# Cross-attention and feed-forward in fp32 on one core: row maxima taken in pairs on half-height matmuls, and the last feed-forward chunk in two halves

## The chip, the cores and the metric

The kernel runs on one NeuronCore of one Trainium2 chip. The metric is the device time of one execution in microseconds (us), lower is better. The median of three runs of the kernel before is 789.1 us (788.37 to 789.65).

## The reference, cut to what matters

Four residual layers are applied one after the other to x (4 x 1024 rows of 256 features), each to a layer-normed input:

```
x = x + attention0(layernorm(x), ctx, mask)   # 16 heads of 16, 77 keys a batch, biases, a mask
x = x + experts(layernorm(x))                 # 6 experts of 128, top 2, tanh gelu
x = x + attention1(layernorm(x), ctx, ctx)    # 16 heads share one key and one value head; q @ k.T / 4
x = x + ffn(layernorm(x))                     # 256 -> 1024 -> 256, piecewise-linear gelu on 33 points,
                                              # values rounded to multiples of 1/256
```

Both attentions use a softmax, so each query row needs its maximum over 77 keys for each head before the exponential.

## The kernel before, in words

The 4096 rows are 8 blocks of 512. A stage runs over all blocks before the next begins: attention 0 (blocks G = 0 to 7), the experts, attention 1 (G = 8 to 15), the feed-forward. Each engine has its own instruction list, written out by hand; semaphores order the engines, and within an engine the order is the program's. All matmuls on the main path split their operands into a leading and a rest part (fp32r) and use three products for one.

A block of attention works like this, with the work for the next block n = G + 1 woven in.

- TensorE makes 16 score tiles (`score`, L400, one for each head, 77 keys x 512 queries). In attention 0 a second matmul (L416) adds the mask. The stationary operand is a stacked key, the moving one a stack of the query's leading part twice, its rest, and minus the row maximum. The maximum is a row of that stack, so no score of block n can start before the row maxima of block n have come in by a DMA (`stack_maxima`, L260, on SyncE's queue).
- ScalarE takes the exponential of each score tile (`exp`, L312).
- TensorE weighs the values (`weigh`, L419): four heads go to four 32-column strips of the array, as 8 matmuls with a 128x32 stationary operand. VectorE turns the result (`unfold`), divides (`divide`) and turns it back (`fold`). TensorE applies the output weights (`output`, L429, 12 matmuls for each half), and VectorE adds to x (`add`).
- For block n, TensorE makes the queries (`queries`, L374, six matmuls for each of two feature halves c), ScalarE and VectorE split them (`leading`, `rest`), and then come 16 units of row maxima (`max_unit`, L378). A unit is one tile of 128 queries against four heads: one matmul of 128x128 against 308 columns (4 heads x 77 keys, from `kblk`, where each head's key stands in its own rows and all other rows are zero), and in attention 0 a second one (L391) that adds the mask. It fills one PSUM bank. VectorE then reduces 308 columns to 4 maxima (`take_maxima`, L335). Units take turns on two banks, `att.X`, so unit u waits until VectorE has taken unit u - 2.
- After the 16 units TensorE turns the maxima (`turn_maxima`, L394, four matmuls), ScalarE copies them (`maxima`, L307) and the DMA puts them into the stack: the next block's first score waits for that.
- The first block of each attention takes its maxima before the loop, over four banks (`FIRST_MAX`, `FIRST_MAX1`).

Within a partition the features are laid out so that rows 0 to 63 hold the even heads of a feature half and rows 64 to 127 the odd ones.

In the feed-forward a block has 8 chunks of 128 hidden features, 64 chunks in all. A chunk k passes: TensorE `hidden`; VectorE `early` (fixed point); ScalarE `gelus` (two activations); GpSimd `climb` (the difference, L721); VectorE `interpolate` (L768); GpSimd `grow` (L728) or VectorE `finish` (the sum); ScalarE `leading` (two activations, L745 and L748); VectorE `rest` (L780); TensorE `output` (12 matmuls, L812). After a block's eight chunks ScalarE rounds (`round_output`), VectorE adds to x (`add`, L789) and SyncE stores the block (L978). The end of the program is this chain for chunk 63 and the store of block 7.

Of the kernel before, what the change touches and what calls it, by code (L numbers as in the profile page):

```python
# [166 lines left out]
class Attention:  # L167


    def __init__(self, nc, sem, place, norm, ps, m):  # L170
        self.nc, self.norm = nc, norm
        self.W, self.X, self.SC, self.U = ps[0:2], ps[2:4], (ps[4], ps[5], ps[7]), ps[6]
# [162 lines left out]
    def take_maxima(self, dve, G, units, banks):  # L335
        for u in units:
            t, c, half = u // 4, u % 4 // 2, u % 2
            dve.wait_ge(self.max_scores, 16 * G + u + 1)
            if u == 0:
                need(dve, self.mt_done, G)  # L340
            out = self.mx[:, t, :].rearrange("q (par c p) -> q c p par", par=2, c=C)[:, c, 2 * half:2 * half + 2, :]
            self.nc.vector.reduce_max(out, banks[u % len(banks)][:, 0:4 * T].rearrange("q (p par t) -> q p par t", p=2, par=2),  # L342
                                      AX.X).then_inc(self.max_taken, 1)
# [34 lines left out]
    def max_unit(self, pe, layer, G, u, banks):  # L378
        t, c, half = u // 4, u % 4 // 2, u % 2
        pe.wait_ge(self.qh_ready, C * G + c + 1)  # L380
        if u == 0:
            need(pe, self.mt_ready, G)
        if u >= len(banks):
            pe.wait_ge(self.max_taken, 16 * G + u - len(banks) + 1)
        bank = banks[u % len(banks)][:, 0:4 * T]
        tile = slice(t * P, (t + 1) * P)
        keys = layer.kblk[:, c % layer.kc, self.batch(G), 4 * half:4 * half + 4, :]
        last = self.nc.tensor.matmul(bank, self.qh[:, c, tile], keys, start=True, stop=not layer.masked)  # L388
        if layer.masked:
            pe.wait_ge(self.mask_ready, 3 * G + 1)  # L390
            last = self.nc.tensor.matmul(bank, self.mh[:, tile], self.id5[:, 0:4 * T], start=False, stop=True)  # L391
        last.then_inc(self.max_scores, 1)

    def turn_maxima(self, pe, G, bank):  # L394
        pe.wait_ge(self.max_taken, 16 * (G + 1))
# [258 lines left out]
class FeedForward:  # L654
# [5 lines left out]
    def __init__(self, nc, sem, place, norm, ps, m):  # L660
# [46 lines left out]
        self.stored = sem("fstored")  # L707

    def wait_y(self, eng, k):

        if k >= 0:
            g, c = divmod(k, FC)
            mine = [j for j in range(FC) if (j in self.ON_DVE) == (c in self.ON_DVE)]
            eng.wait_ge(self.y_ready[c in self.ON_DVE], len(mine) * g + mine.index(c) + 1)

# [34 lines left out]
    def round_output(self, act, g):  # L750
        act.wait_ge(self.used, FC * (g + 1))
        for k in range(2):
            bank = self.OUT[2 * (g % 2) + k]
# [87 lines left out]
def build(nc, d, out):  # L841
    m, at0, at1 = memory_map()
    place = Places(nc)
    with ExitStack() as stack:
# [3 lines left out]
        ps = [stack.enter_context(nc.psum_tensor(f"bank{i}", [P, N], F32)) for i in range(8)]  # L848
# [6 lines left out]
        att = Attention(nc, sem, place, norm, ps, m)  # L855
# [34 lines left out]
        UNITS1 = {1: (0,), 2: (1,), 3: (2,), 4: (3,), 5: (4, 5), 6: (6, 7), 7: (8, 9), 9: (10,), 10: (11,), 11: (14, 15)}  # L890
        FIRST_MAX = (ps[2], ps[3], ps[6], ps[7])
        FIRST_MAX1 = (ps[6], ps[7], ps[2], ps[3])

        with nc.Block() as block:
            @block.sync
            def _(sp):
# [79 lines left out]
                for g in range(BLOCKS):  # L976
                    sp.wait_ge(ff.added, 2 * (g + 1))
                    sp.dma_start(out[:, g * NT:(g + 1) * NT, :], x[:, g * NT:(g + 1) * NT, :]).then_inc(ff.stored, 16)  # L978
                sp.wait_ge(ff.stored, 16 * BLOCKS)

            @block.gpsimd
            def _(pool):
# [120 lines left out]
                for k in range(BLOCKS * FC):  # L1103
                    g, c = divmod(k, FC)
                    ff.climb(pool, k)
# [4 lines left out]
                if FC - 1 not in ff.ON_DVE:  # L1110
                    ff.grow(pool, BLOCKS * FC - 1)

            @block.scalar
            def _(act):
# [22 lines left out]
                att.maxima(act, 0, FIRST_MAX[0])  # L1137
# [12 lines left out]
                for G in range(BLOCKS):  # L1150
                    p, n, nm = G - 1, G + 1, G + 2
                    for h in range(H):
# [3 lines left out]
                        if h == 2 and p >= 0:  # L1156
# [5 lines left out]
                        if h == 5 and p >= 0:  # L1162
                            att.lead_quotient(act, p, 1)
                        if h == 9 and nm <= BLOCKS:
                            norm.norm(act, nm)
                        if h == 12 and n < BLOCKS:
                            att.maxima(act, n, att.X[0])
# [45 lines left out]
                att.maxima(act, BLOCKS, FIRST_MAX1[0])  # L1213
# [3 lines left out]
                for G in range(BLOCKS, 2 * BLOCKS):  # L1217
                    p, n, nm = G - 1, G + 1, LN_ATT1 + G - BLOCKS + 2
                    for h in range(H):
                        att.exp(act, G, h)  # L1220
                        if h < C and n < 2 * BLOCKS:
                            att.leading(act, n, h)
                        if h == 2 and p >= BLOCKS:
# [7 lines left out]
                        if h == 12 and n < 2 * BLOCKS:  # L1231
                            att.maxima(act, n, att.X[0])
# [22 lines left out]
                for k in range(BLOCKS * FC):  # L1255
# [5 lines left out]
                    if k > 0:  # L1261
# [15 lines left out]
                for k in range(BLOCKS * FC - 3, BLOCKS * FC):  # L1277
                    ff.leading(act, k)
                ff.round_output(act, BLOCKS - 1)

            @block.vector
            def _(dve):
# [6 lines left out]
                for c in range(C):  # L1289
                    dve.wait_ge(k_done, c + 1)  # L1290
                    nc.vector.tensor_scalar(l0.kt[:, c, :], FIRST_MAX[2 + c][:, 0:BT], att.cols[:, 1, c:c + 1], DH ** -0.5,
# [14 lines left out]
                att.take_maxima(dve, 0, range(16), FIRST_MAX)  # L1306
# [4 lines left out]
                for G in range(BLOCKS):  # L1311
# [8 lines left out]
                    if n < BLOCKS:  # L1320
                        for c in range(C):
                            att.rest(dve, n, c)
                        att.take_maxima(dve, n, range(0, 2), att.X)
                    if p >= 0:
                        att.unfold(dve, p, 3)
                    if n < BLOCKS:
                        att.take_maxima(dve, n, range(2, 4), att.X)
                    if p >= 0:
                        att.divide(dve, p, 1)
                    if n < BLOCKS:  # L1330
                        att.take_maxima(dve, n, range(4, 6), att.X)
                    if p >= 0:
                        att.fold(dve, p, 1)
                    if n < BLOCKS:
                        att.take_maxima(dve, n, range(6, 10), att.X)
# [3 lines left out]
                    if n < BLOCKS:  # L1339
                        att.take_maxima(dve, n, range(10, 12), att.X)  # L1340
                    if p >= 0:
                        att.add(dve, p, 0)
                    if n < BLOCKS:
                        att.take_maxima(dve, n, range(12, 16), att.X)
                    if p >= 0:
                        att.add(dve, p, 1)
# [426 lines left out]
```

## Time and profile before

| | |
|---|---|
| median of three runs | 789.1 us |
| profiled execution | 788.65 us |
| its span, first to last instruction | 786.4 us |
| PE busy | 730.7 us (93%) |
| DVE busy | 645.4 us (82%) |
| ACT busy | 513.6 us (65%) |
| POOL busy | 374.3 us (48%) |
| mean granted TensorE clock | 0.99 of 2.4 GHz |

PE is TensorE's matmuls, DVE VectorE, ACT ScalarE, POOL GpSimd, SP SyncE. A matmul's row gives a modelled length that is longer than its place in the stream: the distance from one start to the next is what it costs. Attention 0 runs from about 41 to 210 us, attention 1 from about 415 to 577 us, the feed-forward after that.

### The profile page before, as it was taken

The page shows a single profiled execution, that of the slowest core. Times are in us where ns is not written, and L with a number is a line of the kernel's source. Part 1 is how long each engine was busy: PE and PEld are TensorE (multiplying, and loading weights), DVE is VectorE, ACT ScalarE, POOL GpSimd, SP SyncE. Part 2 cuts the span into 40 slices and gives each one's busy share as a digit, 9 for nine tenths or more (in the row PEclk, how much of TensorE's full clock was granted, in tenths as well). Part 3 has the DMA queues.
Part 4 walks back from the last instruction along what each step waited for, and adds up shares of the span by engine and source line. Part 5 has one row for each costly group of instructions (what it writes and reads, how often), then busy time and mean ns, then how long its engine had stood idle before and what let it go on. Part 6 is the DMA issues. An engine that isn't in the chain of part 4 may idle for free.

```text
span 786.4 us, 13553 instructions
## 1 busy us (share of the span) xinstructions
PE 730.7 (93%) x4372; PEld 548.4 (70%) x4372; DVE 645.4 (82%) x1546; ACT 513.6 (65%) x943; POOL 374.3 (48%) x323
## 2 busy tenths in 40 slices
PE   4799999999999999999998999999989999999995
PEld 3456666766558888888875555555558888888985
DVE  7658778777878878888887888998788999999995
ACT  3546556565654456555436777677778989989885
POOL 6374444334222223232214232222259999999884
PEclk9999999999999999999999999999999999999999
DMA  7975635564210000001047755755200000000001
GB/s 231 135 208 121 143 71 96 119 120 87 69 36 1 1 1 7 1 1 55 1 60 121 92 78 77 131 76 78 32 1 1 2 28 28 28 28 2 28 28 54
DMA packets 25101, 48.64 MB, mean 62 GB/s; under 512 B 3686, under 2 KB 7016, under 8 KB 24520
## 3 DMA queue, kind: packets, MB, share of 16 engines
q1 hardware_dynamic: 23366, 46.54, 30.6%
q10 hardware_dynamic: 1666, 1.24, 0.5%
q8 instruction: 36, 0.59, 0.3%
q14 instruction: 33, 0.27, 0.2%
HBM read 12.12 MB, written 4.19 MB: 21 GB/s over the span
## 4 chain that ended last, share of the span: by engine, by line
PE 53%; DVE 20%; issue 9%; ACT 7%; DMA 6%; POOL 4%; DVEq 0%; ACTq 0%; POOLq 0%
PE bank L141 15%; PE bank L649 7%; PE bank L413 6%; PE bank L436 6%; DMA qst<-mt 5%; PE bank L424 5%; PE bank L388 4%; DVE mx L342 4%; PE bank L416 3%; PE bank L812 3%; DVE fpart L768 3%; DVE x L617 2%; PE bank L391 2%; DVE fyl L780 2%; POOL fy L728 2%
## 5 line engine op out<-in xcount | busy, mean ns | idle before, releaser
L316 ACT ACTIVATE pt<-bank 77x512 f32<-77x512 f32 x256 | 141.0, 589 | 79.1 <-PE bank L416 59.3
L342 DVE TENSOR_REDUCE mx<-bank 128x4 f32<-128x308 f32 x256 | 108.6, 470 | 22.9 <-PE bank L391 12.3
L413 PE MATMUL bank<-qst,l_kst 128*77 128x512 f32 (+1 forms) x256 | 102.6, 416 | 16.8 <-DMA qst<-mt 10.5
L721 POOL TENSOR_TENSOR frise<-fg,fg 128x512 f32<-128x512 f32 x64 | 101.8, 1591 | 6.0 <-DVE fpart L768 0.8
L388 PE MATMUL bank<-l_kblk,qh 128*128 128x308 f32 x256 | 81.2, 339 | 7.6 <-DVE mx L342 6.4
L284 POOL TENSOR_TENSOR ol<-ot,oh 128x512 fp32r<-128x512 f32 x32 | 41.4, 1293 | 94.5 <-ACT oh L321 50.4
L103 POOL TENSOR_TENSOR rstd<-var,minus_half 128x4 f32<-128x4 f32 x32 | 34.8, 1088 | 102.5 <-DVE var L98 54.4
L617 DVE SCALAR_TENSOR_TENSOR x<-bank,eweight,x 128x256 f32<-128x256 f32 x192 | 79.5, 475 | 4.5 <-PE bank L649 4.2
L413 PEld LDWEIGHTS bank<-qst,l_kst 128*77 128x77 f32 (+1 forms) x256 | 36.5, 146 | 66.0 <-ACT pt L316 24.1
L114 ACT ACTIVATE xn<-x,shift,rstd 128x256 f32<-128x256 f32 (+1 forms) x128 | 67.0, 592 | 17.9 <-POOL shift L105 17.9
L812 PE MATMUL bank<-fw2h,fyh 128*128 128x256 f32 x256 | 73.3, 286 | 5.0 <-DVE fyl L780 4.7
L388 PEld LDWEIGHTS bank<-l_kblk,qh 128*128 128x128 f32 x256 | 47.6, 190 | 41.3 <-issue 33.6
L728 POOL TENSOR_TENSOR fy<-fpart,fg 128x512 f32<-128x512 f32 x48 | 68.5, 1428 | 9.8 <-DVE fpart L768 6.8
L812 PE MATMUL bank<-fw2l,fyh 128*128 128x256 f32 x256 | 72.0, 281 | 0.0
L812 PE MATMUL bank<-fw2h,fyl 128*128 128x256 f32 x256 | 71.9, 281 | 0.0
L424 PE MATMUL bank<-pt,l_vall 128*32 128x512 f32 x512 | 68.2, 604 | 1.3 <-DVE ut L347 0.9
L768 DVE SCALAR_TENSOR_TENSOR fpart<-ffixed,frise 128x512 f32<-128x512 uint16 x64 | 58.3, 911 | 12.4 <-POOL frise L721 12.4
L649 PE MATMUL bank<-ew2h,ehh 128*128 128x256 f32 x192 | 56.5, 294 | 2.8 <-DVE x L617 2.8
L518 POOL TENSOR_TENSOR ehl<-eh,ehh 128x512 fp32r<-128x512 f32 x16 | 20.7, 1293 | 80.7 <-ACT ehh L534 80.7
L812 PEld LDWEIGHTS bank<-fw2h,fyh 128*128 128x128 f32 x256 | 48.2, 188 | 11.0 <-DVE fyl L780 9.0
L649 PE MATMUL bank<-ew2l,ehh 128*128 128x256 f32 x192 | 54.6, 285 | 0.0
L532 ACT ACTIVATE eh<-bank 128x512 f32<-128x512 f32 x48 | 28.7, 597 | 39.6 <-PE bank L141 38.5
(176 smaller groups left out, 2115.6 us busy)
## 6 DMA issues: line engine op xcount, KB each, us to landing
qst<-qh SPq DMA_DIRECT2D x64, 256.0 KB, 6.5
qst<-ql SPq DMA_DIRECT2D x32, 256.0 KB, 8.7
out<-x SPq DMA_DIRECT2D x8, 512.0 KB, 2.6
qst<-ml SPq DMA_DIRECT2D x8, 480.0 KB
x<-in_x SPq DMA_DIRECT2D x3, 1024.0 KB, 12.7
weights<-in_mlp_w SPq DMA_DIRECT2D x2, 1024.0 KB, 5.2
mraw<-in_mask SPq DMA_DIRECT2D x8, 154.0 KB
x<-in_x SPq DMA_DIRECT2D x2, 512.0 KB, 5.4
```

The lines of the kernel that those rows point to most:

```text
L141: last = self.nc.tensor.matmul(out, w, a, start=(first and k == 0), stop=(k == len(ops) - 1))
L316: self.nc.scalar.activation(self.pt[0:T, i // 4 % 2, i % 4, :], self.bank_of(G, i)[0:T, :], ACT.Exp).then_inc(self.probs, 1)
L342: self.nc.vector.reduce_max(out, banks[u % len(banks)][:, 0:4 * T].rearrange("q (p par t) -> q p par t", p=2, par=2), AX.X).then_inc(self. ...
L388: last = self.nc.tensor.matmul(bank, self.qh[:, c, tile], keys, start=True, stop=not layer.masked)
L413: last = self.nc.tensor.matmul(out, layer.kst[rows, layer.stack(c * HC + 2 * k + par), b * T:(b + 1) * T], self.qst[rows, self.slot(G), c ...
L424: last = self.nc.tensor.matmul(self.U[32 * k:32 * k + 32, :], layer.vall[:, self.batch(G), layer.value(c * HC + 2 * k + par), :], self.pt[ ...
L617: last = self.nc.vector.scalar_tensor_tensor(tile, part, self.weight[:, g % 2, 2 * k + t, e:e + 1], tile, ALU.mult, ALU.add)
L649: last = self.nc.tensor.matmul(self.OUT[k][:, t * D:(t + 1) * D], a[:, e % self.R, tile], w[:, e, :], start=(j == 0), stop=(j == 2))
L721: self.nc.gpsimd.tensor_tensor(self.rise[:, k % 2, :], self.g1[:, k % self.R, :], self.g0[:, k % self.R, :], ALU.subtract).then_inc(self.r ...
L728: self.nc.gpsimd.tensor_tensor(self.y[:, k % 2, :], self.part[:, k % 2, :], self.g0[:, k % self.R, :], ALU.add).then_inc(self.y_ready[0], 1)
L768: self.nc.vector.scalar_tensor_tensor(self.part[:, k % 2, :], self.fractions[:, k % self.R, :, 0], 2.0 ** -16, self.rise[:, k % 2, :], ALU ...
L812: last = nc.tensor.matmul(self.OUT[2 * (g % 2) + t // 2][:, t % 2 * D:(t % 2 + 1) * D], a[:, k % self.R, t * P:(t + 1) * P], w[:, c, :], s ...
```

## The change

- The units become pairs. `max_pair` computes one query tile against eight heads: one matmul on rows 0 to 63 with the four even heads into the first bank of a pair of banks, one on rows 64 to 127 with the four odd heads into the second bank; in attention 0 two full-height mask matmuls follow. VectorE reduces both banks, 616 columns, in one instruction. Eight pairs replace 16 units. The loops have one pair of banks (2 and 3), so pair v waits until pair v - 1 has been taken; before the loops there are two pairs of banks.
- The order of work within the blocks is changed: in attention 0 both query halves come after score 1, the last weighing of the block before after score 3, the first output after score 11, and the third weighing after score 14 instead of 15. In attention 1 the first query half comes ahead of score 0 (for blocks 9 to 14), the first weighing after score 6, and on VectorE the layer norm's rest comes before `fold`.
- Chunk 63 goes through all steps in two halves of 256 columns, with its difference and its sum on VectorE instead of GpSimd; the last block is stored in two parts.

```
-    def max_unit(self, pe, layer, G, u, banks):
-        t, c, half = u // 4, u % 4 // 2, u % 2
+    def max_pair(self, pe, layer, G, v, banks):
+        t, c = divmod(v, C)
...
-        bank = banks[u % len(banks)][:, 0:4 * T]
-        tile = slice(t * P, (t + 1) * P)
-        keys = layer.kblk[:, c % layer.kc, self.batch(G), 4 * half:4 * half + 4, :]
-        last = self.nc.tensor.matmul(bank, self.qh[:, c, tile], keys, start=True, stop=not layer.masked)
+        if v >= len(banks):
+            pe.wait_ge(self.max_taken, 8 * G + v - len(banks) + 1)
+        pair = banks[v % len(banks)]
+        tile = slice(t * P, (t + 1) * P)
+        for par in range(2):
+            half = slice(64 * par, 64 * par + 64)
+            last = self.nc.tensor.matmul(pair[:, par, 0:4 * T], self.qh[half, c, tile],
+                                         layer.kblk[half, c % layer.kc, self.batch(G), 4 * par:4 * par + 4, :],
+                                         start=True, stop=not layer.masked)
         if layer.masked:
-            pe.wait_ge(self.mask_ready, 3 * G + 1)
-            last = self.nc.tensor.matmul(bank, self.mh[:, tile], self.id5[:, 0:4 * T], start=False, stop=True)
+            for par in range(2):
+                last = self.nc.tensor.matmul(pair[:, par, 0:4 * T], self.mh[:, tile], self.id5[:, 0:4 * T], start=False, stop=True)
         last.then_inc(self.max_scores, 1)
...
-            self.nc.vector.reduce_max(out, banks[u % len(banks)][:, 0:4 * T].rearrange("q (p par t) -> q p par t", p=2, par=2),
+            self.nc.vector.reduce_max(out, banks[v % len(banks)][:, :, 0:4 * T].rearrange("q par (p t) -> q par p t", t=T),
                                       AX.X).then_inc(self.max_taken, 1)
...
-        UNITS1 = {1: (0,), 2: (1,), 3: (2,), 4: (3,), 5: (4, 5), 6: (6, 7), 7: (8, 9), 9: (10,), 10: (11,), 11: (14, 15)}
+        PAIRS0 = {2: 0, 3: 1, 6: 2, 8: 4, 11: 5}
+        PAIRS1 = {1: 0, 4: 2, 6: 3, 7: 4, 10: 5, 11: 7}
...
+                        if i == 0 and BLOCKS < G and n < 2 * BLOCKS:
+                            att.queries(pe, l1, n, 0)
                         att.score(pe, l1, G, i)
...
-                for k in range(BLOCKS * FC - 6, BLOCKS * FC):
+                for k in range(BLOCKS * FC - 6, BLOCKS * FC - 1):
                     ff.output(pe, k)
+                for h in range(2):
+                    ff.output_half(pe, h)
...
+                ff.interpolate(dve, BLOCKS * FC - 2)
+                ff.rest(dve, BLOCKS * FC - 4)
+                for h in range(2):
+                    ff.climb_half(dve, h)
+                for h in range(2):
+                    ff.interpolate_half(dve, h)
+                ff.rest(dve, BLOCKS * FC - 3)
+                for h in range(2):
+                    ff.finish_half(dve, h)
+                for i in range(2):
+                    ff.add(dve, BLOCKS - 2, i)
+                ff.rest(dve, BLOCKS * FC - 2)
+                for h in range(2):
+                    ff.rest_half(dve, h)
...
+                for k in range(2):
+                    tiles = slice((BLOCKS - 1) * NT + 2 * k, (BLOCKS - 1) * NT + 2 * k + 2)
+                    sp.wait_ge(ff.added, 2 * (BLOCKS - 1) + k + 1)
+                    sp.dma_start(out[:, tiles, :], x[:, tiles, :]).then_inc(ff.stored, 16)
```

Pairs 3 (after score 6), 6 and 7 of attention 0 and pairs 1 (after score 1) and 6 (after score 10) of attention 1 are called outside these tables: in attention 0 pair 1 comes right behind a weighing, and so does pair 3; in attention 1 pair 0, a weighing and pair 1 follow one another after score 1, pair 3 follows a weighing after score 6, and a weighing follows pair 7 after score 11.

## Rows read from the trace of the kernel before

**Rows 1.** Busy time by window, one block of each attention: window, length, engines.

```profile
109.66:133.96 24.30, 23.82 (x146) 16.14 (x145) 18.69 (x44) 14.34 (x28) 10.21 (x11) 1.00 0.51 98
...
453.71:474.28 20.57, 18.98 (x115) 11.67 (x113) 18.06 (x44) 16.10 (x33) 6.39 (x6) 1.00 0.60 79
```

**Rows 2.** PE's timeline in attention 0, maxima turned to next score: start, us, instruction.

```profile
108.95 0.60 PE L397 MATMUL bank<-ident,mx 128*16 128x128 f32 x4
...
111.74 1.07 PE L424 MATMUL bank<-pt,l_vall 128*32 128x512 f32 x8
113.28 0.46 PE L413 MATMUL bank<-qst,l_kst 128*77 128x512 f32 x1 [0.48 <-DMA qst<-mt]
```

**Rows 3.** PE's timeline in attention 0, units around a weighing.

```profile
97.59 0.30 PE L388 MATMUL bank<-l_kblk,qh 128*128 128x308 f32 x1
97.73 0.30 PE L391 MATMUL bank<-id,mh 128*128 128x308 f32 x1
97.96 1.06 PE L424 MATMUL bank<-pt,l_vall 128*32 128x512 f32 x8
98.96 0.41 PE L388 MATMUL bank<-l_kblk,qh 128*128 128x308 f32 x1
99.20 0.30 PE L391 MATMUL bank<-id,mh 128*128 128x308 f32 x1
```

**Rows 4.** PE's timeline before attention 0: matmuls on one row between full ones.

```profile
29.09 1.03 PE L1518 MATMUL bank<-weights,ctx 128*77 128x256 f32 x4
30.05 0.65 PE L1519 MATMUL bank<-rows,ones_row 1*77 1x256 f32 x2
30.63 1.09 PE L1518 MATMUL bank<-weights,ctx 128*77 128x256 f32 x4
```

**Rows 5.** PE's timeline in the experts: full matmuls, then matmuls on six rows.

```profile
254.86 0.28 PE L649 MATMUL bank<-ew2l,ehh 128*128 128x256 f32 x1
254.98 0.28 PE L649 MATMUL bank<-ew2h,ehl 128*128 128x256 f32 x1
255.19 1.05 PE L632 MATMUL bank<-eanchors,eq 6*128 6x6 f32 x8
```

**Rows 6.** Costliest groups, the reductions of 308 and of 144 columns.

```profile
L342 DVE TENSOR_REDUCE mx<-bank 128x4 f32<-128x308 f32 x256 | 108.6, 470 | 22.9 <-PE bank L391 12.3 <-PE bank L388 9.7
...
L581 DVE TENSOR_REDUCE erank<-eabove 128x24 f32<-128x144 f32 x8 | 2.4, 303 | 0.3
```

**Rows 7.** VectorE's timeline, the first block's 16 units.

```profile
22.36 6.24 DVE L342 TENSOR_REDUCE mx<-bank 128x4 f32<-128x308 f32 x16
```

**Rows 8.** PE's timeline in attention 1, maxima turned to maxima turned.

```profile
453.02 0.60 PE L397 MATMUL bank<-ident,mx 128*16 128x128 f32 x4
...
455.88 0.46 PE L413 MATMUL bank<-qst,l_kst 98*77 98x512 f32 x1
457.27 0.70 PE L413 MATMUL bank<-qst,l_kst 98*77 98x512 f32 x2 [0.93 <-DMA qst<-mt]
...
466.76 0.76 PE L388 MATMUL bank<-l_kblk,qh 128*128 128x308 f32 x2 [0.36 <-DVE mx L342]
...
473.59 0.60 PE L397 MATMUL bank<-ident,mx 128*16 128x128 f32 x4
```

**Rows 9.** The chain of waits, one query half in attention 0: start, us, what.

```profile
89.65 1.36 PE bank L141 x6
```

**Rows 10.** The chain of waits at the end of the program.

```profile
772.51 1.30 POOL frise L721
...
774.57 1.11 POOL fy L728
...
776.97 0.70 DVE fyl L780
...
782.09 0.69 DVE x L789
```

**Rows 11.** DMA issues of the page, the stores of the result.

```profile
out<-x SPq DMA_DIRECT2D x8, 512.0 KB, 2.6
```

More of the change, by code:

```diff
@@ L714, in wait_y, with half, early_half @@
             eng.wait_ge(self.y_ready[c in self.ON_DVE], len(mine) * g + mine.index(c) + 1)
+    def half(self, tile, h):
+        k = BLOCKS * FC - 1
+        return tile[:, k % tile.shape[1], h * (N // 2):(h + 1) * (N // 2)]
+    def early_half(self, dve, h):
+        k = BLOCKS * FC - 1
+        dve.wait_ge(self.hid_done, k + 1)
+        dve.wait_ge(self.part_ready, k - self.R + 1)
+        dve.wait_ge(self.g_ready, k - self.R + 1)
+        self.nc.vector.tensor_scalar(self.half(self.fixed, h), self.HID[k % 2][:, h * (N // 2):(h + 1) * (N // 2)], TO_FIXED, TO_FIXED,
+                                     ALU.add, ALU.subtract).then_inc(self.tail["fixed"], 1)
@@ new lines, in rest_half, with output_half @@
+    def rest_half(self, dve, h):
+        k = BLOCKS * FC - 1
+        dve.wait_ge(self.tail["yh"], h + 1)
+        dve.wait_ge(self.used, k - self.R + 1)
+        self.nc.vector.scalar_tensor_tensor(self.half(self.yl, h), (self.YR[k], self.LN)[h][:, 0:N // 2], TO_256TH,
+                                            self.half(self.yh, h).bitcast(F32), ALU.subtract,
+                                            ALU.subtract).then_inc(self.tail["yl"], 1)
+    def output_half(self, pe, h):
+        k = BLOCKS * FC - 1
+        g, c = divmod(k, FC)
+        pe.wait_ge(self.tail["yl"], h + 1)
+        for t in (2 * h, 2 * h + 1):
+            for a, w in ((self.yh, self.w2h), (self.yh, self.w2l), (self.yl, self.w2h)):
+                last = self.nc.tensor.matmul(self.OUT[2 * (g % 2) + h][:, t % 2 * D:(t % 2 + 1) * D],
+                                             a[:, k % self.R, t * P:(t + 1) * P], w[:, c, :], start=False,
+                                             stop=(t % 2 == 1 and a is self.yl))
+        last.then_inc(self.tail["used"], 1)
@@ L1320, in _ @@
                     if n < BLOCKS:
-                        for c in range(C):
-                            att.rest(dve, n, c)
-                        att.take_maxima(dve, n, range(0, 2), att.X)
+                        att.rest(dve, n, 0)
+                        att.take_maxima(dve, n, range(0, 1), att.X)
+                        att.rest(dve, n, 1)
                     if p >= 0:
@@ L1406, in _ @@
                         att.rest(dve, n, 0)
-                        att.take_maxima(dve, n, range(0, 2), att.X)
-                        att.rest(dve, n, 1)
+                        att.take_maxima(dve, n, range(0, 1), att.X)
                     if p >= BLOCKS:
```

267 lines of the change are left out of this document (154 added, 113 removed).

## The prediction

> **What bounds the kernel now.** I read the windows by block first, then TensorE's timeline through one block of each attention, then the places where TensorE meets a matmul of fewer rows or columns, and last the chain at the end.
>
> In attention 0 TensorE is busy 23.82 of a block's 24.30 us, VectorE only 18.69 [rows 1]. The block is a loop: maxima turned, copied, stacked by DMA, next score, and so on to the next turn. From the turn at 108.95 to the score at 113.28 pass 4.33 us, in which TensorE has other work and idles only 0.48 [rows 2]; the other 19.97 us are TensorE's own stream at its own pace, where a 308-column matmul takes 0.14 (97.59 to 97.73 [rows 3]). So attention 0 pays for every nanosecond that the maxima cost on TensorE, and gains nothing from a faster VectorE.
>
> In attention 1, without mask matmuls, TensorE is busy 18.98 of 20.57 us and VectorE 18.06 [rows 1]. From turn to score TensorE is through at about 456.18 (the score at 455.88 and 0.30) and idles until 457.27; from there to the next turn, 16.3 us, it waits for VectorE in places (0.36 ahead of 466.76) [rows 8]. Here both engines and the DMA share the path.
>
> **The price of a half-height matmul.** This decides the case, and no row shows a 64-row matmul. Rows show what happens when the array's shape changes. Between 128-row matmuls at 0.216 apart ((1.03 - 0.38) / 3, with 0.38 as one's row length), two matmuls on one row: the last full one starts at 29.74, the one-row pair at 30.05, 0.31 later, 0.09 more than its pace; the pair takes 0.58 to the next full one where 0.43 were due, 0.15 more; and the next group is 1.09 long against 1.03, 0.06 more [rows 4]. That is 0.30 for in and out, 0.15 each: 0.09 until the array is empty, 0.06 for a weight load of 77 columns that could not be made ahead. Into six rows it is the same 0.09 (0.21 against 0.12 [rows 5]). Into 32-column strips: 0.23 against 0.14, again 0.09; behind them the first 128-column load shows 0.10 (0.24 against 0.14 [rows 3]). So a change of shape costs about 0.19 with a 128-column load and 0.15 with a 77-column one. The bounds: nothing, if 64 rows are no change of shape, and 0.19 plus a serial second half (0.14 more) if the halves do not overlap. I take 0.19 and overlapping halves, since all three neighbours show the first, and the 8 strip matmuls of a weighing stand within 1.06 us [rows 3], which only side by side they can, at about 0.01 a start. The Trainium skill, "TensorEngine Tiling (Array Packing)", Key Properties, lists two tiles of 64 rows as a mode of their own and says that a switch of mode drains TensorE; by it the price would be that of the neighbours, and no row here shows it for 64 rows.
>
> **Attention 0, maxima.** Before, two units are four matmuls, 0.57. A pair is in 0.19, halves 0.15, out 0.19, two masks 0.29: 0.82, so 0.25 more. Two pairs of eight stand right behind a weighing, whose own way out was paid before: about 0.08 more each. A block: 6 x 0.25 + 2 x 0.08 = 1.66, of which 0.06 goes into waits for VectorE that end. Seven blocks carry pairs in their loop: 7 x 1.6 = **+11.2**. The single pair of banks costs nothing here: one reduction (0.78, below) and its wake-up lie behind at least a score (0.46) and the switch, or a weighing (1.0 [rows 3]), or 12 output matmuls. The moved steps (queries, weighings, transposes) are the same instructions, and none crosses from one side of the turn to the other except the last transposes, which the 0.48 of idle covers: 0.
>
> **VectorE's reductions.** 308 columns take 470 ns, 144 take 303 [rows 6], so 1.02 ns a column, and 616 take 0.78. Back to back they start 0.385 apart ((6.24 - 0.47) / 15 [rows 7]), so one of 616 holds VectorE 0.70 where two held it 0.77. The gain is 0.07 for each pair, not half a reduction. The first blocks are bound by it, 8 x 0.07 = 0.56 each; the first of attention 0 then waits for DMAs, so I count **-0.2**, the second **-0.4**.
>
> **Attention 1.** Putting one query half (1.36 [rows 9]) ahead of score 0 fills the idle: TensorE would be through at 456.18 + 1.36 + 0.03, so score 0 is late by 0.3. It leaves the stretch behind it: -1.36. VectorE gains 5 x 0.07 = 0.35 up to the fifth pair; the last three pairs are in TensorE's own stretch and cost 0.20, 0.20 and 0.05 (in 0.19, halves 0.15, out 0.15, less 0.29; next to a weighing one switch is shared). One pair of banks, where two banks took turns, puts reduction, wake-up, switch and matmul in series where VectorE has nothing else to do, pair 4 behind pair 3 above all: +0.5. Sum 0.3 - 1.36 - 0.35 + 0.45 + 0.5 = about -0.5 a block, 7 blocks **-3.5**; the serial waits are the soft term, and I give a block -1.5 to +0.5. SyncE's queue gets its query copies earlier and nothing else is queued behind new waits; ScalarE's exponential 0 now stands behind the first split, 0.6, which TensorE's two other score banks cover.
>
> **The end.** GpSimd makes difference 63 (1.30) ahead of sum 62 [rows 10]; without it sum 62 comes 1.3 to 1.6 earlier. But VectorE then has four half steps and the two adds of block 6 ahead of `rest` 62, some 2.2 us, so `rest` 62 moves only from 776.97 to about 776.7. Then halves flow: from `rest` to the last add, 5.1 us before (776.97 to 782.09), about 3.6. The last store is 256 KB instead of the 512 KB that takes 2.6 [rows 11], 0.3 less. Sum **-2.3**, between -1 and -3.5.
>
> **Sum.** 11.2 - 3.5 - 0.6 - 2.3 = +4.8 on the profiled 788.65 (span 786.4 and 2.2 around it) is 793.5; the median stands 0.45 above it, so 794.0.
>
> **Rivals.**
> *64 rows change nothing, or the weights are loaded ahead.* The two halves then cost one matmul: a masked pair 0.44 against 0.57, 56 pairs -7.6; in attention 1 the stream is shorter by 0.14 a pair and, with the query half out of the way, a block loses about 1.6, -11; with start and end -2.9: 768. For it: strips do overlap once inside. Against it: each of the rows' three changes of shape was paid. The skill's "TensorE: Matmul & The Clock Gate", Part 3, gives a pack of row tiles the span of one matmul and some 4 ns a tile, with no charge for entering or leaving; by that alone the result would be this one. Chance 0.25.
> *The switch costs half.* If only the 0.09 is paid and the 128-column loads hide behind the neighbour, a masked pair costs 0.62, 56 x 0.05 = +2.6, attention 1 -1.1 a block = -7.7, the rest -2.9: 781. It would need loads across a change of shape, which the 0.06 and the 0.10 speak against. Chance 0.15.
> *The halves run one after the other.* Forecast plus 0.14 in 56 masked pairs and about half as much in attention 1: 794 + 7.8 + 3 = 805. Against it: the strips. Chance 0.04; what is left, 0.56, is the forecast.
>
> **How the numbers follow.** A measurement of this kernel can tell 0.2%, 1.6 us. The forecast's own range is 786 to 800 (attention 1 by -1.5 to +0.5 a block, the end by 1.2 either way); it falls below 787.5 with 0.03, within 0.2% with 0.09, above with 0.44. The first rival and nearly all of the second are faster: 0.25 + 0.14, the second's rest 0.01 the same; the third is slower, 0.04. Faster 0.42, same 0.10, slower 0.48. Since the first rival lies far off, the range to hold 8 in 10 is 766 to 800; the likeliest case's own is 786 to 800.
>
> **What would show it.** Right: in attention 0 blocks of 25.9 us, the distance from the matmul before a pair to its first half 0.09 over the pace, the first mask matmul about 0.34 behind the halves instead of 0.14; reductions of 0.78; attention 1 blocks near 20; VectorE's share of busy time lower. Wrong: blocks of attention 0 under 24.3, or a first half at the normal pace behind its neighbour. The end: the last add about 7 us or less behind sum 62.

## The result and the profile after

The changed kernel takes 809.3 us (median of 4 runs, 806.1 to 810.2) against 788.9 for the kernel before in the same session: 1.0251 times as long, 95% interval 1.022 to 1.0281. The forecast was 794.0 with a range up to 800. The direction was that of the likeliest case (slower had a chance of 0.48); the +4.9 us was a quarter of what came.

The page of the changed kernel: the span, TensorE's busy time and granted clock (in 40 slices), the reductions and the 64-row matmuls.

```profile
span 806.8 us, 13337 instructions
...
PE 754.5 (94%) x4372; PEld 538.4 (67%) x4372; DVE 641.3 (79%) x1425; ACT 513.2 (64%) x947; POOL 371.6 (46%) x321
...
PEclk9679999999999999999998899999999999999999
...
L343 DVE TENSOR_REDUCE mx<-bank 128x8 f32<-128x616 f32 x128 | 101.5, 796 | 52.4 <-PE bank L398 34.0
...
L393 PE MATMUL bank<-l_kblk,qh 64*128 64x308 f32 x256 | 53.5, 410 | 17.0 <-DVE mx L343 14.8
```

One reduction of 616 columns takes 796 ns (forecast 780) where one of 308 took 470 [rows 6]. New are the low figures in the second and third slice of the clock row, 20 to 60 us.

Windows of the changed kernel, columns as in [rows 1] (busy time of PE, its weight loads, DVE, ACT, POOL, then granted clock, DMA share, GB/s). In order: the start of the first block's trouble, the rest of that block, one steady block of attention 0, attention 1's first two blocks, and a steady one.

```profile
25.90:49.70 23.80, 22.91 (x59) 11.96 (x59) 8.85 (x29) 6.04 (x11) 12.68 (x20) 0.50 0.84 168
49.70:70.19 20.49, 17.95 (x84) 9.51 (x83) 10.34 (x17) 9.56 (x18) 11.23 (x11) 0.92 0.55 113
147.77:173.63 25.86, 25.55 (x147) 15.18 (x145) 18.41 (x36) 14.29 (x29) 10.26 (x9) 1.00 0.47 92
431.77:455.10 23.33, 19.02 (x83) 11.03 (x84) 15.09 (x33) 13.01 (x24) 8.02 (x8) 0.79 0.72 106
455.10:477.15 22.05, 20.95 (x115) 12.39 (x114) 17.02 (x35) 15.20 (x29) 5.07 (x5) 0.90 0.56 74
497.22:517.33 20.11, 19.02 (x115) 10.56 (x113) 17.80 (x38) 15.01 (x31) 5.08 (x5) 1.00 0.62 81
```

And the kernel before, the first block of attention 0 and the first two of attention 1:

```profile
29.30:60.14 30.84, 26.22 (x125) 16.12 (x124) 14.88 (x44) 15.50 (x29) 24.00 (x30) 0.94 0.91 182
...
413.60:433.10 19.50, 16.74 (x83) 10.69 (x84) 14.85 (x40) 12.80 (x23) 8.06 (x8) 0.94 0.78 120
433.10:453.70 20.60, 19.03 (x115) 11.72 (x114) 18.09 (x44) 15.20 (x30) 5.11 (x5) 1.00 0.65 85
```

The steady blocks came close to the forecast: 25.86 for 25.9, and 20.11 for "near 20". Each block runs from one copy of the turned maxima to the next, and between these marks the 20.4 us by which the spans differ are:

| stretch | measured | forecast |
|---|---|---|
| up to the first turned maxima (29.3 to 32.4) | +3.1 | -0.2 |
| attention 0, first block (30.8 to 37.8) | +6.9 | +1.6 |
| attention 0, its next six blocks | +8.4 | +9.6 |
| from there to attention 1's first turned maxima | -0.3 | -0.4 |
| attention 1, first and second block | +3.8, +1.5 | -0.5, -0.5 |
| its next five | -1.5 | -2.5 |
| behind them | -1.5 | -2.3 |

The runs of steady blocks come within 1.2 us of the forecast in each attention. The surplus, some 15 us, lies in the start and in three blocks, all with a lower granted clock than before: 0.73 over the whole first block of attention 0 (before 0.94), 0.79 (0.94) and 0.90 (1.00) in attention 1's first two.

How it begins, in TensorE's timeline of the changed kernel (start, us, instruction, idle time before it): pairs ahead of attention 0, then the value matmuls behind them.

```profile
24.26 0.41 PE L393 MATMUL bank<-l_kblk,qh 64*128 64x308 f32 x2
...
25.32 0.41 PE L393 MATMUL bank<-l_kblk,qh 64*128 64x308 f32 x2 [0.17 <-DVE mx L343]
...
27.68 0.63 PE L393 MATMUL bank<-l_kblk,qh 64*128 64x308 f32 x2
...
29.05 0.62 PE L393 MATMUL bank<-l_kblk,qh 64*128 64x308 f32 x2
...
32.19 1.91 PE L1626 MATMUL bank<-weights,ctx 128*77 128x256 f32 x4
...
44.04 1.97 PE L127 MATMUL bank<-ident,xn 128*128 128x128 f32 x8
```

Up to 25.3 a pair takes 0.8 us, waits apart; from 25.9 the clock stands at its lower level (1.2 GHz, granted 0.50), pairs come 1.37 apart and wait for nothing, and the value matmuls take 11.85 us (32.19 to 44.04). It is back at 2.4 GHz only at 49.7.

### The profile page after: what moved, and what is told of

It is laid out like the page before. It is cut to its first block, busy times and chain, and to the rows that moved or that the text cites. A ratio compares the mean times of both kernels' runs of the same rounds, so it can differ in the third digit from the quotient of the medians.

```text
span 806.8 us, 13337 instructions
## 1 busy us (share of the span) xinstructions
PE 754.5 (94%) x4372; PEld 538.4 (67%) x4372; DVE 641.3 (79%) x1425; ACT 513.2 (64%) x947; POOL 371.6 (46%) x321
## 4 chain that ended last, share of the span: by engine, by line
PE 60%; DVE 18%; issue 8%; ACT 5%; POOL 4%; DMA 4%; ACTq 0%; DVEq 0%; POOLq 0%
PE bank L141 15%; PE bank L431 7%; PE bank L420 6%; PE bank L656 6%; PE bank L443 6%; PE bank L393 5%; PE bank L398 4%; PE bank L423 3%; DMA qst<-mt 3%; DVE mx L343 3%; PE bank L894 3%; DVE fpart L850 2%; DVE x L624 2%; PE bank L127 2%; DVE fyl L862 2%
## 5 line engine op out<-in xcount | busy, mean ns | idle before, releaser
L343 DVE TENSOR_REDUCE mx<-bank 128x8 f32<-128x616 f32 x128 | 101.5, 796 | 52.4 <-PE bank L398 34.0
L420 PE MATMUL bank<-qst,l_kst 128*77 128x512 f32 (+1 forms) x256 | 99.9, 425 | 4.5 <-DMA qst<-mt 2.9
L103 POOL TENSOR_TENSOR rstd<-var,minus_half 128x4 f32<-128x4 f32 x32 | 34.9, 1092 | 107.4 <-DVE var L98 60.6
L393 PEld LDWEIGHTS bank<-l_kblk,qh 64*128 64x128 f32 x256 | 26.1, 188 | 71.3 <-issue 61.0
L808 POOL TENSOR_TENSOR fy<-fpart,fg 128x512 f32<-128x512 f32 x47 | 66.5, 1415 | 9.7 <-DVE fpart L850 6.8
L420 PEld LDWEIGHTS bank<-qst,l_kst 128*77 128x77 f32 (+1 forms) x256 | 35.6, 147 | 53.0 <-ACT pt L317 23.8
L393 PE MATMUL bank<-l_kblk,qh 64*128 64x308 f32 x256 | 53.5, 410 | 17.0 <-DVE mx L343 14.8
L656 PE MATMUL bank<-ew2h,ehl 128*128 128x256 f32 x192 | 54.6, 284 | 0.0
```

Of the source, the lines that this page charges most:

```text
L343: self.nc.vector.reduce_max(out, banks[v % len(banks)][:, :, 0:4 * T].rearrange("q par (p t) -> q par p t", t=T), AX.X).then_inc(self.max_ ...
L393: last = self.nc.tensor.matmul(pair[:, par, 0:4 * T], self.qh[half, c, tile], layer.kblk[half, c % layer.kc, self.batch(G), 4 * par:4 * pa ...
L420: last = self.nc.tensor.matmul(out, layer.kst[rows, layer.stack(c * HC + 2 * k + par), b * T:(b + 1) * T], self.qst[rows, self.slot(G), c ...
L656: last = self.nc.tensor.matmul(self.OUT[k][:, t * D:(t + 1) * D], a[:, e % self.R, tile], w[:, e, :], start=(j == 0), stop=(j == 2))
```

## The experiments

**Full rows again.** Theory A, my forecast's, with what the traces added: changing to 64 rows costs 0.25 us a masked pair, and the holes it leaves let the clock fall. Theory B: the ring of two banks and the order cost.

```diff
-            half = slice(64 * par, 64 * par + 64)
+            half = slice(0, P)
```

The second kernel has this in attention 0 alone (`if layer.masked`), the third only in the eight pairs ahead of each loop (`if len(banks) == 2`).

> The changed kernel with both matmuls of a pair taking all 128 rows of queries and keys again (the keys of the other halves are zero there), everything else as changed: two banks, one reduction of 616 columns, the new order, the new end. Theory A (64-row matmuls cost 0.25 us a masked pair because the array changes its shape, and the gaps that this leaves let the granted clock fall in the first block and in attention 1's first blocks): attention 0's blocks fall from 25.85 to between 24.2 and 24.6 us, the spell at 0.5 from 25.9 to 49.7 us shrinks to one like those of before (3.5 us) or vanishes, the first activation of maxima comes near 29.5 us instead of 32.4, and the kernel takes 780 to 788 us. Theory B (halves cost little; two banks as one ring, one reduction for both and the new order are what costs): blocks stay at 25.5 or more, the long spell stays, and the kernel takes 804 us or more.

> The changed kernel with full 128-row matmuls in attention 0's pairs alone (its first maxima included), 64-row ones in attention 1. Theory A: attention 0 as in the kernel with full rows everywhere; attention 1's blocks as in the changed kernel (20.1 us, and 22 to 23 for the first two if the clock still falls there); the kernel takes 2 to 5 us more than with full rows everywhere if the gaps behind 64-row pairs draw attention 1's low clock, and within 1 us of it if that comes from the order. Theory B: 804 us or more.

> The changed kernel with full 128-row matmuls only in the eight pairs ahead of each attention's loop, 64-row ones inside both loops. Theory A with the clock lost in these eight pairs: the spell from 25.9 to 49.7 us is cut to some 3.5 us, first block from 37.8 back to near 32.4 (30.85 of before and 1.55 for its masked pairs), the first activation of maxima at 29.5 to 30 us, attention 0's later blocks stay at 25.85, and the kernel takes 797 to 802 us. If the clock falls because of what stands behind these pairs (order, waits, transfers) or by chance, the spell stays and the time is 806 us or more.

Measured: everywhere 790.9 us, 1.0025 (1.0016 to 1.0035) of before; attention 0 alone 793.7, 1.0052 (1.0036 to 1.0068); ahead of the loops 802.7, 1.017 (1.0155 to 1.0185). Windows with full rows everywhere, attention 0, attention 1's first block, a steady one:

```profile
113.79:138.20 24.41, 24.04 (x147) 16.01 (x145) 18.24 (x36) 14.20 (x28) 10.60 (x11) 1.00 0.51 98
...
417.96:442.38 24.42, 19.59 (x83) 12.10 (x84) 15.22 (x33) 13.21 (x24) 8.03 (x8) 0.78 0.68 101
462.49:482.36 19.87, 18.43 (x115) 11.43 (x113) 17.66 (x36) 16.06 (x32) 6.39 (x6) 1.00 0.62 82
```

The 64 rows cost 25.86 - 24.41 = 1.45 us a block: theory A, by size too. With full rows ahead of the loops alone the window from the first turned maxima is

```profile
30.78:63.56 32.78, 27.38 (x125) 15.39 (x124) 13.91 (x35) 15.41 (x29) 23.95 (x30) 0.95 0.83 174
```

so 5 us of the first block come back, with the clock, from pairs that end before the block begins, and 1.7 us ahead of it (30.78 for 32.44): 6.6 of the 8.6 us of surplus there. The 802.7 us are just above the 797 to 802 that I expected.

Full rows in attention 0 alone cost 2.8 us over full rows everywhere, within theory A's 2 to 5: attention 1's second block takes 22.2 us with 64 rows and 20.1 without, the later ones 0.2 more each, while its first is no slower (23.6 against 24.4). But 780 to 788 was missed: with full rows everywhere attention 1's first block still takes 24.4 us against 19.5, and attention 0's first 34.9. So theory B has a share, in the first blocks. Each profile is one execution: the first two kernels run the same code up to there, and yet take 34.9 and 33.2 us for attention 0's first block, so pieces of it under some 2 us are not resolved.

**The end alone**: the kernel before with the feed-forward's last chunk in halves and the last store in two parts, attention untouched.

```diff
+                for h in range(2):
+                    ff.output_half(pe, h)
...
+                for k in range(2):
+                    tiles = slice((BLOCKS - 1) * NT + 2 * k, (BLOCKS - 1) * NT + 2 * k + 2)
```

> The kernel before with the change's end alone: the last chunk of the feed-forward in two halves and the last block's store in two parts; attention as before. The change's trace has 1.5 us less behind the last activation of maxima than before (228.4 against 229.95), of which the forecast had given 2.3 to the end. If that is the end's own doing: 787.0 to 787.8 us, 1.1 to 1.9 below before. If the halves merely replace one wait by another: within 0.5 us of before.

Measured 787.7 us, 0.9977 (0.9968 to 0.9987), 1.6 us under before. The chain at the end of the changed kernel shows why not 2.3:

```profile
799.16 0.69 DVE fyl L862
...
799.89 1.69 PE bank L894 x12
801.58 0.73 PE bank L791 x6
...
802.39 0.59 ACT bank L836
...
803.00 1.34 DVE x L871 x2
```

From `rest` 62 to the last add starting (half of the x2, 803.67) are 4.5 us, before 5.1 [rows 10]: 0.6 gained, 1.5 forecast. Both halves stand behind chunk 62's 12 output matmuls, so the first half gains nothing. `rest` 62 itself came 0.3 later (counted from the last turned maxima), and the shorter store gave 1.2 (from the last add's end to the end of the span 2.5 us, before 3.6).

**Pairs or order.** I made the kernel before with the new end and, in attention 1 from its second block on, the new arrangement with full rows: once with pairs, once with two single-bank matmuls and two reductions of 308 columns in each pair's place. In a third, the changed kernel itself got single banks and full rows everywhere; its edit of `max_pair`, in part:

```diff
+            if v >= len(banks):
+                pe.wait_ge(self.max_taken, 16 * G + 2 * (v - len(banks)) + par + 1)
...
-        last.then_inc(self.max_scores, 1)
+            last.then_inc(self.max_scores, 1)
```

> The kernel before with the change's end, and with the change's arrangement of attention 1 from its second block on: pairs with one reduction of 616 columns, first query half ahead of the scores, but full 128-row matmuls. Attention 0 and attention 1's first block keep single banks. With full rows everywhere the later blocks of attention 1 took 19.88 us against 20.57 before, and attention 1's first block 24.4 against 19.5. Theory C (one ring of two banks costs where VectorE has little else to do, the first block; pairs gain 0.6 to 0.7 us in each of the later ones): first block 19.5, five of the next six at 19.9, the kernel 4 us under the one with the new end alone, 783 to 785 us. Rival: the gain of the later blocks only repays what the first block lost (work put off there is done later): later blocks at 20.4 or more, 787 us or more.

> As the kernel with late pairs, but each pair's place in the order holds two single-bank matmuls with a reduction of 308 columns each: the new order without the pairs. Theory C1 (the gain of attention 1's later blocks comes from fewer, longer reductions): blocks at 20.3 to 20.6 us, the kernel near the one with the new end alone, 786.5 to 788 us. Theory C2 (it comes from the query half ahead of the scores, which covers the 0.93 us wait before score 0): blocks at 19.7 to 20.0, the kernel at 783 to 785 us.

> The changed kernel's order and end with full rows and with each bank reduced for itself (16 reductions of 308 columns a block, each bank refilled as soon as its own is taken), in place of one reduction over two banks. Theory C: the first block of attention 1 comes down from the 24.4 us it took with full rows and pairs to 20 to 21 us, and its spell of low clock goes; attention 0 within 0.3 us a block of 24.4; the kernel takes 786 to 789 us, 2 to 5 under the one with full rows and pairs. Rival (the order costs the first blocks, not the ring): attention 1's first block stays at 23 us or more.

Measured: late pairs 785.8 us, 0.9954 (0.9938 to 0.997); the same order with single banks 783.3, 0.9914 (0.9901 to 0.9927); single banks everywhere 781.9, 0.9891 (0.9874 to 0.9908). A steady block of attention 1, late pairs:

```profile
474.23:494.21 19.98, 18.42 (x115) 11.41 (x113) 17.75 (x38) 15.00 (x30) 5.07 (x5) 1.00 0.62 82
```

The same, single banks in the new order:

```profile
474.13:493.56 19.43, 19.02 (x115) 11.57 (x113) 17.98 (x46) 15.01 (x30) 5.08 (x5) 1.00 0.64 83
```

Single banks everywhere: attention 0, attention 1's first block, a steady one.

```profile
109.53:133.62 24.09, 23.77 (x147) 16.09 (x145) 18.58 (x44) 14.19 (x28) 10.59 (x11) 1.00 0.52 99
...
412.45:434.89 22.44, 19.80 (x83) 12.00 (x84) 15.49 (x41) 13.05 (x24) 8.05 (x8) 0.81 0.73 109
...
473.52:492.83 19.31, 18.92 (x115) 11.57 (x113) 17.96 (x46) 14.93 (x31) 5.10 (x5) 1.00 0.64 84
```

The whole gain of attention 1's steady blocks comes from the order, and the 0.93 us of idle time ahead of score 0 [rows 8] is gone in both late kernels, as C2 had it; the other moves of the order were not run apart from it. The paired reduction is a loss wherever I tried it. With the pair VectorE has 0.2 us less to do in a block and the block is 0.55 longer. Late pairs came above their 783 to 785 us. Single banks everywhere came below their 786 to 789, but attention 1's first block, at 22.4 us, fits neither theory C (20 to 21) nor its rival (23 or more): the order and the ring both cost there.

The cost of the pair is plainest in VectorE's timeline where it has least else to do, in attention 1's first block. In that of the kernel with full rows and pairs:

```profile
427.39 0.80 DVE L343 TENSOR_REDUCE mx<-bank 128x8 f32<-128x616 f32 x1 [0.59 <-PE bank L393]
428.89 0.80 DVE L343 TENSOR_REDUCE mx<-bank 128x8 f32<-128x616 f32 x1 [0.70 <-PE bank L393]
```

and in the kernel before:

```profile
425.34 0.86 DVE L342 TENSOR_REDUCE mx<-bank 128x4 f32<-128x308 f32 x2 [0.77 <-PE bank L388]
426.38 0.87 DVE L342 TENSOR_REDUCE mx<-bank 128x4 f32<-128x308 f32 x2 [0.18 <-PE bank L388]
```

One pair takes 1.50 us a round, because matmuls and reduction alternate on the same two banks; two units take 1.04, since one bank fills while the other is read.

**Filler.** Behind each of the eight pairs ahead of attention 0 two 128-row matmuls into a bank that is overwritten later; they are extra work, and everything else is as changed.

```diff
+        if len(banks) == 2 and layer.masked:
+            for k in range(2):
+                self.nc.tensor.matmul(self.SC[0][:, 0:4 * T], self.qh[:, c, tile],
+                                      layer.kblk[:, c % layer.kc, self.batch(G), 0:4, :], start=True, stop=True)
```

> The changed kernel, 64-row matmuls everywhere, with two extra 128-row matmuls of 308 columns behind each of the eight pairs ahead of attention 0's loop, into a bank that is overwritten later; they compute nothing that is used and add 2.3 us of work at full clock (16 of 0.144). Theory A2 (the clock fell because TensorE stood too much in these pairs): the spell of 25.9 to 49.7 us shrinks to one of some 3.5 us, first block from 37.8 to near 32.5 us, and the kernel is 3 to 6 us faster than the changed one in spite of the extra work, 803 to 806 us. Rival (the change of the array's shape itself draws the low clock, or the waits behind the pairs do): the spell stays, the extra work costs 2 to 5 us, 811 us or more.

Measured 808.3 us (805.6 to 811.5), 1.0233 (1.0205 to 1.0262), which the clock cannot be read from: the interval covers that of the changed kernel. The trace can. The same stretch of TensorE's timeline:

```profile
28.78 0.41 PE L393 MATMUL bank<-l_kblk,qh 64*128 64x308 f32 x2
29.12 0.55 PE L398 MATMUL bank<-id,mh 128*128 128x308 f32 x2
29.51 0.45 PE L402 MATMUL bank<-l_kblk,qh 128*128 128x308 f32 x2
...
31.00 1.03 PE L1630 MATMUL bank<-weights,ctx 128*77 128x256 f32 x4
...
37.34 1.09 PE L127 MATMUL bank<-ident,xn 128*128 128x128 f32 x8
```

With 2.3 us more work the value matmuls start 1.2 us earlier and take 6.34 us instead of 11.85; the first low spell behind the pairs is at 49.6 to 53.0. So in this execution the clock held through the same eight pairs, with as many changes of shape; the change of shape alone does not lose it. The four executions took 805.6, 805.7, 810.8 and 811.5 us, and the trace is of the 805.7; where the clock fell in the longer two is not known (their mean granted clocks are 0.975 and 0.977, the changed kernel's 0.965 to 0.975). My 803 to 806 us was missed: two later spells stand where the changed kernel had one, the first block takes 35.5 us and not 32.5, and of attention 1's spells one has moved from the second block to the third, which takes 21.6 us for 20.1.

**Twice the changes of shape, the sum of the good parts, and the changed kernel again.** The kernel with single banks, but each 64-row matmul followed by its own 128-row mask matmul:

```diff
+            half = slice(64 * par, 64 * par + 64)
-            last = self.nc.tensor.matmul(pair[:, par, 0:4 * T], self.qh[:, c, tile],
-                                         layer.kblk[:, c % layer.kc, self.batch(G), 4 * par:4 * par + 4, :],
+            last = self.nc.tensor.matmul(pair[:, par, 0:4 * T], self.qh[half, c, tile],
+                                         layer.kblk[half, c % layer.kc, self.batch(G), 4 * par:4 * par + 4, :],
```

> The changed order with single banks (as in the kernel with single banks), but 64-row matmuls, and in attention 0 each is followed by its own 128-row mask matmul: 16 changes to 64 rows a block and 16 back, where the changed kernel has 8 each way. Theory A (each entry and each return has its price): one unit costs 0.09 us before the 64-row matmul, 0.19 before its mask matmul and some 0.1 behind it, 0.38 in all; 16 of them 6.1 us, of which the pairs of the changed kernel paid three quarters on the path (0.18 of 0.25 us a pair): blocks of 28 to 29 us in attention 0 (27 to 30), against 24.05; attention 1, without masks, within 0.4 us of 19.3. Rival (the 64-row matmuls are dear because two of them share the array, not because it changes shape): blocks below 25.5 us.

Measured 842.7 us, 1.0673 (1.0629 to 1.0717). Its block of attention 0, and two of its units:

```profile
137.07:166.97 29.90, 29.58 (x147) 16.95 (x145) 19.57 (x44) 14.29 (x28) 10.60 (x11) 1.00 0.42 80
```

```profile
150.52 0.41 PE L394 MATMUL bank<-l_kblk,qh 64*128 64x308 f32 x1
150.86 0.41 PE L398 MATMUL bank<-id,mh 128*128 128x308 f32 x1
151.20 0.40 PE L394 MATMUL bank<-l_kblk,qh 64*128 64x308 f32 x1
```

A unit takes 0.68 us (150.52 to 151.20) where two full matmuls take 0.29, and (29.90 - 24.09) / 16 = 0.36 us each land on the block. The price is that of the change of shape. Attention 1's steady blocks, at 20.0 us, are 0.7 over those with full rows, where I had allowed 0.4. It brought the worst start of all, with the lower clock from 21.3 to 55.4 us.

The next is the kernel before with the change's order (except in attention 1's first block) and its end, single banks and 128 rows throughout: the change without its pairs.

> The kernel before with the change's order in attention 0 and in attention 1 from its second block on, with the change's end, and with single banks, full 128-row matmuls and reductions of 308 columns throughout; attention 1's first block keeps the order of before. If orders and end are what the change brings and the parts add up: attention 0's blocks 24.05 us (as with single banks in the changed kernel), attention 1's first block 19.5 to 19.8, the later ones 19.4, and the kernel 778 to 781 us, 1 to 4 under the kernel with single banks everywhere. Rival: what attention 1's first block lost to the new order was only shifted between it and its neighbours: 781.5 us or more.

Measured 781.0 us (781.0 to 781.2), 0.9891 (0.9875 to 0.9908): **it beats both kernels**, by 8.5 and 28 us. Attention 0, attention 1's first block:

```profile
109.42:133.51 24.09, 23.81 (x147) 16.10 (x145) 18.56 (x44) 14.18 (x28) 10.59 (x11) 1.00 0.52 99
...
412.29:431.72 19.43, 16.59 (x84) 10.55 (x85) 14.85 (x40) 12.84 (x23) 8.06 (x8) 0.95 0.79 121
```

The first block's old order is worth 3.0 us there (22.44 against 19.43), but the next block takes 0.7 more (19.95 against 19.29) and the ends differ; the total cannot be told from that of single banks everywhere.

> The changed kernel once more, unedited, for a second profile. If the long spell at the lower clock (25.9 to 49.7 us) belongs to the kernel, it is there again within a few us, with a first block of 37 to 38 us and 806 to 810 us in all. If it was this one execution's chance, the spell is some 3.5 or 7 us long, and the first block 33 to 36 us.

Measured 810.6 us, 1.0254 (1.0228 to 1.028). The long spell is there again, and longer:

```profile
21.10:51.80 30.70, 29.55 (x78) 16.00 (x79) 13.60 (x36) 8.11 (x12) 12.85 (x21) 0.50 0.76 155
```

The first block takes 37.7 us, attention 1's first two 23.3 and 22.1. The long spell belongs to the kernel, its start does not: here the clock is at 0.50 before the first pair, behind 3.35 us in which TensorE waits for `kblk`, so the pairs did not bring it down. They did not bring it back either. The kernel with full rows ahead of the loops met the same wait and the same low clock, and was back at full speed by 24.8 us. The first pair of the changed kernel in its second profile, then the first and the fourth pair with full rows:

```profile
21.35 0.63 PE L393 MATMUL bank<-l_kblk,qh 64*128 64x308 f32 x2 [3.35 <-DVE l_kblk L1398]
```

```profile
21.32 0.88 PE L393 MATMUL bank<-l_kblk,qh 128*128 128x308 f32 x2 [3.36 <-DVE l_kblk L1398]
...
24.80 0.45 PE L393 MATMUL bank<-l_kblk,qh 128*128 128x308 f32 x2
```

Over all profiles, the spell in this stretch is 24 to 34 us long where the first maxima are taken with 64-row matmuls and no filler (the changed kernel twice, the alternating one once); in each of the others no spell up to 60 us is longer than 7.

## Why the prediction was wrong

**The price of a change of shape** held. A pair of the changed kernel, in TensorE's timeline:

```profile
114.08 0.39 PE L423 MATMUL bank<-mm,id 128*77 128x512 f32 x1
114.40 0.41 PE L393 MATMUL bank<-l_kblk,qh 64*128 64x308 f32 x2
114.74 0.55 PE L398 MATMUL bank<-id,mh 128*128 128x308 f32 x2
115.13 0.28 PE L443 MATMUL bank<-l_woh,oh 128*128 128x256 f32 x1
```

The first half starts 0.32 behind the score's mask, 0.09 over its pace of 0.23; the halves start together; the masks follow 0.33 to 0.34 later. Forecast: 0.09 and 0.34. The three rivals fall with it: the price is not zero (768), not half (781), and the halves are not serial (805), though 805 lies nearer to the 809.3 measured than 794 does. "TensorE: Matmul & The Clock Gate", Part 3, in the Trainium skill gives a pack of row tiles one matmul's span and some 4 ns a tile: inside the pack the trace agrees (two halves have a length of 0.41 us, as one alone has at 150.52 in the alternating kernel), but entry and exit cost 0.39 us a pair here, 0.25 more than the packing saves, and each entry and exit of the alternating kernel costs 0.39 again.

**Attention 0's steady blocks**: +1.56 for 1.6, by parts that I had partly wrong. 64 rows +1.45; the ring, "costs nothing here", +0.3 (24.41 against 24.09); the order, 0 in the forecast, -0.2 (24.09 against 24.30 [rows 1]).

**Attention 1's steady blocks**: -0.46 for -0.5 (-0.3 as the mean of the last five), again by errors that cancel. The order gave -1.1 to -1.3 (20.57 [rows 1] to 19.43 and 19.31; forecast 0.3 - 1.36). The ring and the paired reductions together cost +0.55, forecast -0.35 + 0.5. The 64 rows cost 0.24 (20.11 against 19.87), forecast 0.45.

**The end**: -1.5 to -1.6 for -2.3, inside its bounds. "Then halves flow" was the part that failed: they queue behind chunk 62's output matmuls, and 0.6 came for 1.5. `rest` 62 came 0.3 later instead of 0.3 earlier, and the store gave 1.2 where 0.3 stood. Those three forecast terms add up to 2.1, not to the 2.3 that went into the sum.

**The failed step** is what the forecast said of the first blocks: "-0.2" and "-0.4" for the reductions, and else the steady blocks' price. Three things were missing there.
1. The ring. In attention 1's first block VectorE has little else to do, so a round of matmuls and reduction stands bare: 1.50 us instead of 1.04. I had priced this for the steady blocks of attention 1 alone, and taken the first blocks as bound by VectorE.
2. The order. In attention 1's first block it costs 3.0 us (22.44 against 19.43), part of it clock (granted 0.81 against 0.95).
3. The clock. I carried every matmul at full speed, and read the granted clock of before (0.99) as a fact of the machine, not as something that the edit could change. In the changed profile the granted clock stands at 0.50 for 47.8 us, in that of before for 13.7 (the last microseconds apart). The 23.8 us from 25.9 on are the largest piece: the value matmuls alone take 5.5 us more in it than the same ones did in the filler's run, and full rows in the eight pairs ahead of the loops gave back 6.6 us of the whole. Time at 0.50 is no measure by itself: the fastest kernel here, the order and the end alone, has 23.9 us of it.

Of attention 1's first block (19.50 to 23.33) the order alone gave +3.0, the ring +2.0 (24.42 against 22.44), and the 64 rows -1.1 (23.33 against 24.42).

Waits on the banks alone did not lose the clock. The Trainium skill, in the same page's "A second HAM failure mode: psum-queue depth-cycling", describes small idle times between groups of matmuls, from cycling through PSUM banks, that make the clock fall and return. The changed trace fits it only in part: the clock falls at 25.9 us, while no idle time in the pairs ahead of it, from 22 us on, is over 0.41 us. The same pairs of banks with full rows everywhere waited longer and more often, and kept the clock:

```profile
23.41 0.52 PE L393 MATMUL bank<-l_kblk,qh 128*128 128x308 f32 x2 [0.72 <-DVE mx L343]
...
25.19 0.53 PE L393 MATMUL bank<-l_kblk,qh 128*128 128x308 f32 x2 [0.28 <-DVE mx L343]
```

The filler's run kept it too, with 64-row matmuls and no wait recorded between the pairs. Of these runs, only those with 64-row matmuls and no filler ahead of attention 0 lost the clock there for long. What in them does so is not shown.

What stays open: how the surplus in each of the slow blocks divides between waits and clock. Full rows, single banks, filler and order each changed both together. The filler's first block kept 3 us over what I expected; full rows in attention 0 took 33.2 and 34.9 us there with pairs and 31.3 with single banks, so the ring is a likely part of it, which no run with the filler tells.

## What to carry to other kernels

Price an edit of a tightly filled engine in its thin stretches apart from the steady ones: ask there what the edit does to the granted clock, since here eight pairs whose own price was 2 us stood at the head of 24 to 31 us of half speed. Two banks that take turns are worth more than one reduction over both; a longer instruction that saves 0.07 us of start-up lost here, where producer and consumer alternate on its buffer. And when an edit bundles a reordering with a new shape, run them apart: here order and end together were worth 8.5 us, and the pairs with their 64 rows cost 27 (809.3 against 781.9 with single banks and full rows).

## What the runs showed of the hardware that I had not expected

Once at 0.50, the clock stayed there while TensorE's records show it busy for 22.91 of 23.80 us: value matmuls with one-row matmuls between them did not bring it back; it came back at 49.7, 4 us into a stretch of score and query matmuls. With the same value matmuls entered at full clock, it held. Entered low at 21.3 us, full-row pairs had it back by 24.8; entered low at 21.1, eight 64-row pairs ended at 32 us with it still low. And one way in and out of 64 rows costs the same 0.39 us in both kernels: in the changed kernel a pair holds TensorE 0.82 us (from 0.23 behind 114.08 to 115.13), of which the halves, side by side, are 0.14 and the masks 0.29; in the alternating kernel a unit holds it 0.68, of which the two matmuls are 0.29.
